# Waits for constant values without a count, in a four-layer graph network on one core

## The chip, the cores and the metric

The kernel runs on 1 core of one Trainium2 chip. The metric is the device time of one execution in microseconds. It is taken on runs of the kernel as it is; one more execution is profiled, and its trace gives all rows below.

## The reference

12,500 nodes with 48 features each, 400,000 edges sorted by destination, with 48 features and a weight each. Four residual layers, each on `h = max(layernorm(x), 0)`:

```
x += segment_sum(edge_weight * h[src -> gathered at dst], src) @ W + bias      # L0: gather at dst, sum by src
x += (1 + eps) * h + segment_sum(relu(h[src] + edge_attr), dst)                # L1: gather at src, sum by dst
x += A (A h)          # L2: A = D^-1/2 (edges + loops) D^-1/2, by src, two passes
x += A' h             # L3: the same normalised adjacency, transposed
```

## The kernel before, in words

Every engine has its own instruction stream, written out by hand, and streams meet only through semaphores. The fast path has four stages.

Stage A (60 to 5,900 us of the span) reads the edges once and sorts them. A chunk K (53 of them) is 60 columns of 128 edges, in three slots s of 20 columns. For each slot TensorE counts edges per block of 128 source nodes (`count`, L2174), gathers node features (`pick`, two halves, L2186) and ranks edges in their block (`rank`, four quarters, L2195 and L2197). VectorE weighs the gathered features into `rec` (`weigh`, L1737), reads the ranks (`highest`, L1732) and computes each edge's place (`positions`, L1754). GpSimd then scatters the 20 columns of `rec` to the DRAM table `recB` with 20 indirect DMAs (`scatter`, L1420), one for each 128 edges. Buffers `rec`, `qpos` are three deep, one for each slot number; `slot_free` (L1340) waits for the scatters of slot (K-1, s) before slot (K, s) is written.

Beside this, the buckets of the chunk before (10 groups g of 10 blocks) are read back. TensorE sums messages by node (L2212 to L2216) and counts pairs of nodes into a dense matrix, in five pieces for each group (`bucket`, L2204; the matmuls into `pT`, L2230 and L2234, two banks in turn, piece e waits for the copy of piece e-2). ScalarE copies each piece to `stg` (L2585) after a wait on `e_ca` (L2584), and after five copies stores them with a DMA (L2590). SyncE loads the buckets, features and rows with DMAs of its own.

The loops over K, s and g of stage A are unrolled in Python, so that all their wait values are constants. GpSimd's scatters are interrupted by waits on TensorE: `paced` (before columns 2, 4, 6, ... of a slot, on piece numbers by the table `PACE`) and `ranked` (before two or three columns, on `e_rk`, by `RANKED`). These two, and the waits on positions, weights, edge rows and prefilled memory at the head of `scatter`, all go through `hold`.

Stage B (5,915 to 7,240 us) is layer 1 on the sorted edges: TensorE gathers and sums, VectorE adds and makes one-hots, ScalarE and GpSimd split numbers into three bf16 pieces. Its loop over K is a hardware loop on all engines but TensorE, so its waits are mostly against register values. Stages C and D (7,240 to 9,072 us) are dense matmuls with the counted adjacency (`dense`, L2332, with `hold` on the loaded columns; `product`, L2362).

`hold` (L230) is called where an engine must wait before its next step: on GpSimd in `scatter`; on ScalarE in `make_dT`, `bucket`, `meta`; on SyncE before nearly every DMA; on VectorE in `slot_free`; on TensorE in `dense`. Other waits in the file are `wait_ge` alone, through `reached` (L1346) or directly. `general_...` functions are a slow path for other inputs that isn't run here.

Of the kernel before, what the change touches and what calls it, by code (L numbers as in the profile page):

```python
# [92 lines left out]
def build(nc, x, src, dst, ea, ew, weight, bias, eps, out):  # L93
    with ExitStack() as ctx:
# [3 lines left out]
        def sem(name):  # L98
            return ctx.enter_context(nc.semaphore(name))
# [84 lines left out]
        s_hold = sem("s_hold")  # L184
# [44 lines left out]

        def hold(eng, sem_, val):  # L230

            eng.wait_ge(sem_, val).then_inc(s_hold, 1)

        def cols(ap, i, g):
            return ap[:, bass.ds(i * TL + g * G, G)]
# [51 lines left out]
        def general_gpsimd(p):  # L287
# [23 lines left out]
            with p.If(fl):  # L311
                with p.Fori(0, MI) as i:
                    for g in range(L):
                        n = i * L + g
                        p.wait_ge(f_st, n * 2 + 2)
                        hold(p, f_ea, n * 16 + 16)
                        for k in range(G):
                            p.indirect_dma_start(recT, bass.IndirectOffsetOnAxis(ap=posi[:, g, k:k + 1], axis=0),
                                                 rows[:, g, k * RW:(k + 1) * RW], None).then_inc(s_fd, 16)
                        p.wait_ge(s_fd, n * 80 + 80)  # L320
                        p.sem_inc(f_sc, 1)
# [7 lines left out]
            with p.Fori(0, NI) as i:  # L329
                for g in range(L):  # L330
                    n = i * L + g
                    p.wait_ge(b_msg, n + 1 + L)
                    p.wait_ge(b_rc, n + 1)
                    hold(p, b_pi, n + 1)
                    for k in range(G):
                        p.indirect_dma_start(recN, bass.IndirectOffsetOnAxis(ap=posi[:, g, k:k + 1], axis=0),
                                             rows[:, g, k * RW:(k + 1) * RW], None,
                                             bounds_check=E - 1, oob_is_err=False).then_inc(s_cr[g], 16)
# [11 lines left out]
            def gather(k, i, g):  # L350
                S, q = WHICH[k]
                if S is main:
                    q -= 1
                hold(p, S["ix"], (i + q * NI) * L + g + 1)
                for c in range(G):
                    p.indirect_dma_start(gb[:, g, c * D:(c + 1) * D], None, tab[k],
                                         bass.IndirectOffsetOnAxis(ap=posi[:, g, c:c + 1], axis=0)
                                         ).then_inc(S["g"][g], 16)
# [696 lines left out]
        val = pha("val", [128, SB], F32)  # L1055
# [1953 lines left out]
```

## Time and profile before

| | |
|---|---|
| median of 3 runs | 9079.17 us (9056.56 to 9087.81) |
| profiled execution | 9074.16 us |
| its span | 9072.3 us |
| stage A, 60 to 5,855 us | 5795 us of it |
| TensorE busy | 6311.8 us (70%), 98,024 matmuls |
| VectorE, ScalarE, GpSimd busy | 57%, 40%, 46% |
| granted TensorE clock, mean of the span | 0.79 |

A line of the profile page's digits shows the span in 40 slices, and each digit is the busy share of a slice in tenths:

```profile
PE   5555555555555555555555555579999899999999
...
POOL 2455555555555555555555555568888600000000
PEclk6677666676666667666666676799999999999999
```

In the rows an engine's name with a q (ACTq, SPq, POOLq) is its sequencer: waits, branches and the issue of DMAs. "remote" and "another core or an unknown queue" stand for a wait whose end the profile can't tie to an instruction; the kernel has one core, so no other core is meant.

### The profile page before, as it was taken

How to read it: one execution, taken by the hardware profiler on the slowest of the kernel's cores; microseconds unless marked ns; L12 is line 12 of the kernel's file. 1: busy time of each engine (PE TensorE's matmuls, PEld its weight loads, DVE VectorE, ACT ScalarE, POOL GpSimd, SP SyncE). 2: the span in 40 equal slices, each digit the busy share in tenths (PEclk: the TensorE clock that was granted, in tenths of full speed). 3: DMA queues.
4: the chain of work that ended last, by engine and by line, in shares of the span. 5: the costliest groups of instructions: out<-in, count | busy, mean ns of one | idle time of the engine just before them, and what ended most of it. 6: DMA issues, size and time to landing. Idle time of an engine off the chain costs nothing.

```text
span 9072.3 us, 246452 instructions
## 1 busy us (share of the span) xinstructions
PE 6311.8 (70%) x98024; PEld 5439.8 (60%) x98025; DVE 5135.0 (57%) x7430; ACT 3658.8 (40%) x6626; POOL 4155.1 (46%) x4228
## 2 busy tenths in 40 slices
PE   5555555555555555555555555579999899999999
PEld 4444444444444444444444444468888899999999
DVE  5555555555555555555555555599999911111565
ACT  3444444444444444444444444478888600000000
POOL 2455555555555555555555555568888600000000
PEclk6677666676666667666666676799999999999999
DMA  6666566666666666666665666579999987888998
GB/s 172 186 180 179 177 181 183 183 187 179 190 183 181 177 179 200 182 177 181 191 185 177 185 190 184 162 251 316 316 318 316 306 272 261 283 276 277 283 266 213
DMA packets 1540180, 1969.31 MB, mean 217 GB/s; under 512 B 620045, under 2 KB 1204095, under 8 KB 1538767
## 3 DMA queue, kind: packets, MB, share of 16 engines
q1 hardware_dynamic: 1064800, 1272.38, 47.4%
q10 hardware_dynamic: 374342, 523.47, 18.5%
q0 software_dynamic: 100000, 158.60, 5.6%
q8 instruction: 776, 12.71, 0.6%
q14 instruction: 262, 2.15, 0.1%
HBM read 1335.36 MB, written 618.65 MB: 215 GB/s over the span
## 4 chain that ended last, share of the span: by engine, by line
PE 41%; another core or an unknown queue 17%; issue 13%; DVE 12%; ACT 10%; ACTq 2%; DMA 2%; POOL 2%; SPq 0%; DVEq 0%; POOLq 0%
PE pG L2347 9%; PE pT L2230 7%; PE pG L2374 7%; ACT stg L2585 5%; PE pT L2234 3%; PE pG L2186 3%; DVE doh L1724 2%; PE pT L2347 2%; ACT dfar L2552 2%; PE pR L2347 2%; DVE msum L1936 2%; PE pG L2197 2%; PE pG L2195 1%; PE pG L2311 1%
## 5 line engine op out<-in xcount | busy, mean ns | idle before, releaser
L1420 POOL DMA_INDIRECT recB<-rec,qpos x3125 | 3071.8, 983 | 2782.7 <-PE pT L2230 1376.0
L2230 PE MATMUL pT<-soh,doh 128*128 128x128 bf16 x10600 | 1820.9, 269 | 1608.3 <-ACT stg L2585 1317.4
L2585 ACT CAST stg<-pT 128x512 fp8e4<-128x512 f32 x2650 | 1497.7, 585 | 1977.5 <-PE pT L2230 1147.4
L2230 PEld LDWEIGHTS pT<-soh,doh 128*128 128x128 bf16 x10600 | 1042.5, 118 | 1867.8 <-ACT stg L2585 1421.5
L2234 PE MATMUL pT<-car,qidb 128*128 128x256 fp8e4 x2597 | 932.9, 359 | 32.5 <-issue 32.0
L1732 DVE TENSOR_REDUCE val<-pG 128x5 f32<-128x490 f32 x628 | 417.6, 665 | 878.7 <-PE pG L2197 385.4
L1737 DVE TENSOR_TENSOR rec<-pG,wN 128x480 f32<-128x480 f32 x314 | 206.6, 658 | 1173.2 <-remote 1053.1
L2311 PE MATMUL pG<-mpl,doh 128*128 128x144 bf16 x10388 | 765.9, 227 | 38.6 <-POOL mpl L1471 28.7
L1724 DVE TENSOR_TENSOR doh<-dm,pG 128x2560 bf16<-128x2560 bf16 x530 | 783.7, 1479 | 3.0 <-ACT dm L2671 2.6
L1724 DVE TENSOR_TENSOR doh<-smd,pG 128x2560 bf16<-128x2560 bf16 x530 | 783.4, 1478 | 0.0
L1724 DVE TENSOR_TENSOR soh<-smd,pG 128x1280 bf16<-128x1280 bf16 x530 | 432.5, 816 | 514.9 <-PE pT L2230 376.8
L2311 PEld LDWEIGHTS pG<-mpl,doh 128*128 128x128 bf16 x10388 | 666.8, 96 | 68.6 <-POOL mpl L1471 52.4
L2195 PE MATMUL pG<-ohA,qlt 128*128 128x490 bf16 x628 | 307.0, 489 | 562.1 <-DVE val L1732 435.0
L2374 PE MATMUL pG<-xq,yt 128*128 128x144 bf16 x9800 | 615.7, 226 | 13.0 <-DMA xq<-hS 8.6
L2374 PEld LDWEIGHTS pG<-xq,yt 128*128 128x128 fp8e4 x9800 | 615.0, 98 | 13.6 <-issue 8.8
L1468 POOL TENSOR_TENSOR mpl<-mpl 128x480 f32<-128x480 f32 x530 | 523.5, 988 | 200.8 <-ACT mpl L2696 198.0
L1476 POOL MEMSET xi<- 64x512 bf16 x1 | 0.5, 519 | 1221.0 <-PE pT L2347 1221.0
L2010 DVE TENSOR_REDUCE ysC<-pG 128x144 f32<-128x432 f32 (+1 forms) x50 | 24.6, 541 | 938.8 <-PE pG L2347 485.4
L2299 PE MATMUL pG<-xp,sT 128*128 128x48 bf16 x15582 | 485.1, 183 | 101.8 <-ACT sT L2686 52.3
L1471 POOL TENSOR_TENSOR mpl<-mpl 128x480 f32<-128x480 f32 x530 | 523.6, 988 | 41.4
L2556 ACT ACTIVATE dT<-dfar,qonf 128x1280 bf16<-128x1280 bf16 x314 | 427.5, 1362 | 274.4 <-remote 248.1
L2299 PEld LDWEIGHTS pG<-xp,sT 128*128 128x128 bf16 x15582 | 443.9, 96 | 148.4 <-ACT sT L2686 99.6
(265 smaller groups left out, 14180.2 us busy)
## 6 DMA issues: line engine op xcount, KB each, us to landing
recB<-zt ACTq DMA_DIRECT2D x102, 2425.5 KB
brec<-recB SPq DMA_DIRECT2D x477, 495.0 KB
erec<-recB SPq DMA_DIRECT2D x477, 495.0 KB, 5.5
cl<-cA SPq DMA_DIRECT2D x80, 2560.0 KB, 10.9
cA<-stg ACTq DMA_DIRECT2D x530, 320.0 KB
cl<-cA SPq DMA_DIRECT2D x40, 2720.0 KB, 11.2
drow<-dlD SPq DMA_DIRECT2D x157, 640.0 KB
srowB<-srD SPq DMA_DIRECT2D x265, 320.0 KB, 5.9
```

What stands on the lines that cost most here:

```text
L1420: p.indirect_dma_start(recF, bass.IndirectOffsetOnAxis(ap=qpos[:, s, c:c + 1], axis=0), rec[:, s, c, :], None).then_inc(s_sc[s], 16)
L1468: p.tensor_tensor(mpl[:, o, 1, :, :], mpl[:, o, 0, :, :], mpl_u[:, o, 0, :, :, 1], ALU.subtract).then_inc(m_r1, 1)
L1471: p.tensor_tensor(mpl[:, o, 2, :, :], mpl[:, o, 1, :, :], mpl_u[:, o, 1, :, :, 1], ALU.subtract).then_inc(m_pl, 1)
L1724: return v.tensor_tensor(out.rearrange("p b (c two) -> p b c two", two=2), code.unsqueeze(2).to_broadcast([128, n, w // 2, 2]), numbers[:, ...
L2230: ins = t.matmul(bank[:, h * 256 + b * 128:h * 256 + b * 128 + 128], doh[:, o, 2 * e + b, h * 128:(h + 1) * 128], soh[:, o, 2 * e + b, :], ...
L2234: t.matmul(bank[:, 0:256], qidb[:, :], carf[:, r, e * 256:(e + 1) * 256], start=False, stop=True, skip_group_check=True)
L2299: ins = t.matmul(B8[o][:, b * D:(b + 1) * D], sT[:, g % 5, b * 128:(b + 1) * 128], xp[:, g * GB + b, k, :], start=(k == 0), stop=(k == 2))
L2311: ins = t.matmul(B8[2 + 2 * par][:, h * 3 * D:(h + 1) * 3 * D], doh5[:, g % 5, b, h * 128:(h + 1) * 128], mpl_u[:, g % 2, :, b, :, 1], sta ...
L2347: ins = t.matmul(B8[4 * o + b // 3][:, b % 3 * 3 * D:(b % 3 + 1) * 3 * D], clf[u % 3][:, k, b * 128:(b + 1) * 128], (xpc, xw)[r][:, k0 + k ...
L2374: ins = t.matmul(B8[o][:, w * 3 * D:(w + 1) * 3 * D], ytf[o][s][:, n, w * 128:(w + 1) * 128, b], xq[:, FIRST[s] + n, b, :], start=(s == 0 ...
L2556: a.activation(dT[:, half], dfar[:, :], ACT.Relu, bias=qonf[:, 0:1], scale=-1.0).then_inc(e_dT, 1)
L2585: a.copy(stg[:, o, :, e * 256:(e + 1) * 256], B8[6 + (g * 5 + e) % 2][:, :].rearrange("p (h x) -> p h x", h=2), saturate=False).then_inc(e ...
```

## The change

`hold` so far made a wait that also adds 1 to the semaphore `s_hold` when it is over. Nothing waits for `s_hold`. Now this is so only where the value is held in a register; where it is a Python integer, the wait is a `wait_ge` like the others, with nothing added. All calls, values and their order stay, `paced` and `ranked` on GpSimd among them.

```diff
         def hold(eng, sem_, val):
 
-            eng.wait_ge(sem_, val).then_inc(s_hold, 1)
+            if isinstance(val, int):
+                eng.wait_ge(sem_, val)
+            else:
+                eng.wait_ge(sem_, val).then_inc(s_hold, 1)
```

The callers that matter most:

```
def paced(K, s, c):
    back, g = SUMMED[s][1]
    hold(p, e_ca, ((K - back) * JG + g) * 5 + PACE[s][c])
...
for e in range(5):                                  # ScalarE, bucket
    hold(a, e_ca, c * 5 + (e + 1))
    a.copy(stg[...], B8[6 + (g * 5 + e) % 2][...]).then_inc(e_cv, 1)
hold(a, e_cv, c * 5 + 5)
a.dma_start(cA[...], stgB[...]).then_inc(s_cs[o], 16)
```

## Rows read from the trace of the kernel before

**Rows 1.** Windows, three stages: span, busy time (instructions) per engine, granted clock, DMA share, GB/s.

```profile
60.00:5855.00 5795.00, 3262.42 (x42267) 2475.19 (x42267) 3167.79 (x5216) 2545.97 (x4879) 3070.30 (x3124) 0.68 0.62 181
...
5915.00:7240.00 1325.00, 1179.90 (x26127) 1103.13 (x26128) 1309.46 (x1431) 1039.28 (x1607) 1049.36 (x1062) 0.98 0.94 307
7240.00:8470.00 1230.00, 1213.92 (x19375) 1213.20 (x19372) 216.52 (x368) 14.28 (x26) 1.50 (x3) 1.00 0.86 273
```

**Rows 2.** Chain of waits from 60 to 5900 us: share of it by line.

```profile
by line: another core or an unknown queue 26.2%; issue 14.2%; PE pT L2230 11.4%; ACT stg L2585 7.3%; PE pT L2234 4.1%; PE pG L2186 4.0%; ACT dfar L2552 3.7%; PE pG L2197 2.5%; PE pG L2195 2.2%; DVE doh L1724 2.0%; PE pG L2174 1.8%; DVE rm L
```

**Rows 3.** Waits from 60 to 5900 us: who waited for whom, us, times, longest.

```profile
POOL recB L1420 <- PE pT L2230: 1376.0, 472, 8.7
...
ACT stg L2585 <- PE pT L2230: 1146.2, 1357, 9.4
...
DVE rec L1737 <- remote: 1053.1, 188, 10.7
...
ACT hs L2539 <- remote: 405.8, 87, 7.1
...
DVE val L1732 <- remote: 384.0, 74, 11.2
```

**Rows 4.** Waits of the held line 232 on its own: kind, count, ns min/median/max, stretch.

```profile
L232 ACTq EVENT_SEMAPHORE  x4447: 17/17/1392, 42.4 to 5914.1; - x194
L232 SPq EVENT_SEMAPHORE  x3941: 2/17/4119, 68.5 to 8416.4; - x198
L232 POOLq EVENT_SEMAPHORE  x2260: 17/17/17, 78.2 to 5841.7; - x189
...
L232 PEldq EVENT_SEMAPHORE  x138: 51/51/164, 7227.6 to 8431.1; - x138
```

**Rows 5.** The copies as a group (page, part 5); one beside TensorE (timeline).

```profile
L2585 ACT CAST stg<-pT 128x512 fp8e4<-128x512 f32 x2650 | 1497.7, 585 | 1977.5 <-PE pT L2230 1147.4
...
3052.89 0.42 PE L2230 MATMUL pT<-soh,doh 128*128 128x128 bf16 x2
...
3053.42 0.58 ACT L2585 CAST stg<-pT 128x512 fp8e4<-128x512 f32 x1 [3.21 <-PE pT L2230]
```

**Rows 6.** ScalarE, VectorE and TensorE where the wait has no count.

```profile
3051.04 1.38 PE L2186 MATMUL pG<-hw,dT 128*128 128x48 bf16 x30
...
3052.46 0.66 DVE L1737 TENSOR_TENSOR rec<-pG,wN 128x480 f32<-128x480 f32 x1 [0.34 <-PE pG L2186]
...
6498.45 0.65 DVE L1936 TENSOR_TENSOR msum<-pG,erec 128x480 f32<-128x480 f32 x1
...
6499.14 0.60 ACT L2696 ACTIVATE mpl<-msum 128x480 f32<-128x480 f32 x1 [0.95 <-DVE msum L1936]
...
6499.82 0.99 POOL L1468 TENSOR_TENSOR mpl<-mpl 128x480 f32<-128x480 f32 x1 [0.59 <-ACT mpl L2696]
```

**Rows 7.** GpSimd and ScalarE released by one matmul, and the pick beside them.

```profile
1988.83 0.93 PE L2186 MATMUL pG<-hw,dT 128*128 128x48 bf16 x30
...
1988.74 1.07 ACT L2585 CAST stg<-pT 128x512 fp8e4<-128x512 f32 x2 [0.92 <-PE pT L2230]
...
1989.43 0.96 POOL L1420 DMA_INDIRECT recB<-rec,qpos  x1 [1.07 <-PE pT L2230]
```

**Rows 8.** The run of scatters from 3040 us, and what starts after it.

```profile
3041.74 1.38 PE L2186 MATMUL pG<-hw,dT 128*128 128x48 bf16 x30
...
3046.43 0.96 POOL L1420 DMA_INDIRECT recB<-rec,qpos  x1 [0.30 <-issue]
3048.64 0.66 DVE L1737 TENSOR_TENSOR rec<-pG,wN 128x480 f32<-128x480 f32 x1 [9.92 <-remote]
```

**Rows 9.** Head of a slot: positions written, then the first scatter.

```profile
3028.54 0.18 DVE L1754 TENSOR_TENSOR qpos<-posf,nowhere 128x20 int32<-128x20 f32 x1
...
3030.01 0.95 POOL L1420 DMA_INDIRECT recB<-rec,qpos  x1 [3.80 <-issue]
```

**Rows 10.** Chain of waits over the span, by engine (the page).

```profile
PE 41%; another core or an unknown queue 17%; issue 13%; DVE 12%; ACT 10%; ACTq 2%; DMA 2%; POOL 2%; SPq 0%; DVEq 0%; POOLq 0%
```

## The prediction

> **What bounds the kernel now.** I read the windows first. Stage A takes 5795 of 9072 us, and there no engine is full: TensorE is busy 3262 us, GpSimd 3070, VectorE 3168, at a granted clock of 0.68 [rows 1]. In stage B VectorE is busy 1309 of 1325 us, in stage C TensorE 1214 of 1230 [rows 1]. So a change in how engines hand work to one another can show in stage A, and hardly elsewhere.
>
> Second, the chain of waits of stage A. 26.2% of its 5840 us, 1530 us, is "an unknown queue", 7.3% (426 us) are ScalarE's copies L2585, 14.2% is "issue", the time between a release and a start [rows 2]. The list of waits tells what the unknown part is: VectorE waits 188 times for L1737, 74 times for L1732 and ScalarE 87 times for L2539, together 349 waits and 1843 us, mean 5.3 us [rows 3]. All three wait for TensorE's matmuls. A close look shows such a case: the 30 matmuls of a `pick` end at 3041.74 + 1.38 = 3043.12, yet the VectorE operation that waits for them starts at 3048.64, 2.21 us after the start of the last scatter of a run on GpSimd that had begun before [rows 8]. When GpSimd stood still the same step took 0.04 us (matmuls end at 3052.42, VectorE starts at 3052.46) [rows 6]. So a signal of TensorE that falls into a run of scatters is often told only when the run is over. I don't know by which path; but it says what the `paced` and `ranked` waits do, they break the runs, and it makes the start of each run matter.
>
> (1) ScalarE's copies. With a hold: TensorE's last matmul of a piece ends at 3052.89 + 0.42 = 3053.31, the copy starts at 3053.42, 0.11 us [rows 5]. Without: 0.04 us on VectorE after `pick` and 0.04 us on ScalarE itself after VectorE (6499.10 to 6499.14) [rows 6]. The hop gets 0.07 us shorter. The chain holds 426 / 0.585 = 728 copies (585 ns is their mean [rows 5]). If all of them were released by TensorE, that is 51 us; before 1357 of the 2650 ScalarE stood idle for it [rows 3, 5], 51%, which gives 26 us. I take 40.
>
> (2) GpSimd's paced scatters. A single matmul releases ScalarE, which starts 1988.74, and GpSimd, which starts 1989.43, 0.69 us later [rows 7]; with ScalarE's own 0.11 us the hop is 0.80 us. Of it 0.30 us stand before every scatter, waiting or not [rows 8]. GpSimd's hop without a count, on an arithmetic instruction, is 0.08 us (6499.74 to 6499.82) [rows 6]. The trace shows no indirect DMA with a wait of its own, so the saving lies between 0 and 0.80 - 0.08 = 0.72 us. I take 0.80 - 0.30 - 0.08 = 0.4. What is it worth? 1530 us of unknown waits at 5.3 us are some 290 on the chain. Each ends with a run, and the run ends earlier by what it starts earlier, if its start is what was late. GpSimd waited for a piece of TensorE 472 times [rows 3], and I take it that for half of the 290 such a start is what was late: 290 x 0.4 x 0.5 = 58, I take 60. Ends: 0 and 290 x 0.72 = 209 us.
>
> The Trainium skill, Perfetto Trace Analysis, section on GPSIMD's SWDGE instructions, says that the sequencer pushes such an instruction into a wait queue with its wait and is then free to decode the next. By that rule the whole decoding of a scatter could be over before its wait is, and the sum would take the upper end of (2) rather than its middle. No row of this trace has that case; an indirect DMA never carries a wait here.
>
> (3) Heads of slots. At a head six holds stand in a row on GpSimd for s = 0 and four for s = 1, 2. The positions are ready at 3028.72, the first scatter starts at 3030.01, 1.29 us, 0.49 more than (2) has for one hold [rows 9], so 0.1 us for each of five further ones. Half of them go, 0.25 us, at 157 heads 39 us, and 0.4 us more at each by (2), 63 us. But GpSimd is only 2% of the chain [rows 10], and in two of three slots (the run before still goes on) the waits are over long before. I take 15; ends 0 and 80.
>
> (4) DMAs issued on ScalarE. Before each store of a group there is a hold on the copies. ACTq is 2% of the chain [rows 10], 181 us, at 0.38 us an issue some 470; 0.07 us each is 33 us. The instructions between the wait and the DMA stay. I take 20; ends 0 and 33.
>
> (5) At nothing: SyncE's holds (3941) shorten every load by 0.06 us or so, but SPq is 0% of the chain [rows 10]; if its loads ran late, 0.06 us on 530 bucket loads would be 32 us. VectorE's waits on free slots, and TensorE's 138 in stage C, where matmuls already issued cover them (TensorE is busy 1214 of 1230 us [rows 1]); without the cover 138 x 0.07 = 10 us. In stage B almost all held values are in registers and stay as they are. The 8600 or so updates of `s_hold` that go away are waited for by nobody.
>
> **Sum.** 40 + 60 + 15 + 20 = 135 us. These hops run beside others that are nearly as late: a copy that comes 0.07 us sooner may then wait for a landing or for the end of a run. I take a quarter off: 101 us. 9074 - 101 = 8973 for the profiled execution, and 9079 - 101 = 8978 against the median, which lies 5 us above it: 8975. All upper ends together (51 + 209 + 80 + 33) would give 8706.
>
> **Rivals.**
>
> *Scatters start sooner and catch more signals (slower).* The pacing tables count TensorE's pieces, and what lies between a piece and the start of a scatter is the 0.80 us of part (2). With 0.4 us less, the `pick`, `rank` or `count` that TensorE does right after the piece ends inside the run more often. The case is there: a `pick` runs from 1988.83 to 1989.76, and the run of scatters that a piece before it released began at 1989.43, 0.33 us before its end [rows 7]. The price of one signal caught is a scatter and a half, 1.3 to 2 us; more where the run is long, as the 5.5 us of [rows 8]. If each chunk catches two more, at 1.7 us, that is 53 x 2 x 1.7 = 180 us, less the 75 of parts (1), (3) and (4): 9079 + 105 = 9184. It decides from about one more caught signal a chunk (90 us) on. For it: the 1530 us of unknown waits are of this kind. Against it: the runs also end sooner, and many signals are already caught.
>
> *Absorbed (no change).* The ends of runs set the beat of stage A, and ScalarE's 0.07 us wait for it like the rest. If GpSimd's hop stays as it is, only a small part of (1) and (4) is left, 20 us: 9059. For it: 26% of the chain ends with a run. Against it: 7.3% are copies, which wait for no run.
>
> *The waits stay instructions of their own (the change doesn't do what it says).* Then 17 ns each and the updates alone go: 9070 to 9079. Against it: waits without a count start 0.04 us after the release in three rows [rows 6].
>
> *The whole of GpSimd's hop goes (faster still).* Part (2) at its upper end and runs broken at better places: 9079 - 250 = 8829.
>
> **How the numbers follow.** Within 0.3% (27 us) a measurement of this kernel can't be told from no change. Chances: forecast 0.50 (8880 to 9040), more signals caught 0.26 (9110 to 9260), absorbed 0.15 (9045 to 9085), waits stay 0.02, faster still 0.07. Faster: 0.50 + 0.07 + 0.04 of the absorbed = 0.61; no change 0.13; slower 0.26. The likeliest case's own range is 8880 to 9040; the range for all is 8830 to 9160, which leaves out some 0.03 below and 0.17 above.
>
> **What would show it right or wrong.** The list of waits on line 232 shrinks by most of its 10,800 entries. ScalarE's L2585 starts 0.04 us after a piece, not 0.11. The hop from ScalarE's start to GpSimd's at one release shrinks from 0.69 to about 0.3 us. "Unknown queue" falls by 40 to 60 us in stage A and stages B to D keep what they have (9072 - 5915 = 3157 us). If GpSimd's hop has shrunk and the unknown waits have grown in number or length, the first rival holds; if neither L2585's hop nor GpSimd's has changed, I was wrong about what a count costs. A stage B or C that moves by over 20 us would mean that I looked at the wrong place.

## The result: 9083 to 8921 us, and the profile after

The changed kernel takes 8920.94 us in the median of 4 runs (8911.64 to 8932.20); the kernel before took 9083.49 beside it (4 runs). The ratio is 0.9826 [0.9801, 0.9851], 162.6 us less. In a second set beside other kernels it was 8925.15 against 9085.96, ratio 0.9829 [0.9806, 0.9852], 160.8 us less. Forecast were 8975 us, from a gain of 101 us. Direction and range were right, and the gain was 1.6 times the forecast one.

The profiled span went from 9072.3 to 8913.6 us, 158.7 less. First the windows of the changed kernel (columns as in [rows 1]):

```profile
60.00:5700.00 5640.00, 3206.33 (x42245) 2438.38 (x42245) 3171.17 (x5216) 2548.73 (x4877) 3068.27 (x3118) 0.69 0.63 186
...
5760.00:7080.00 1320.00, 1177.75 (x26094) 1098.87 (x26095) 1307.11 (x1429) 1040.53 (x1608) 1048.72 (x1062) 0.98 0.94 308
7080.00:8310.00 1230.00, 1216.10 (x19410) 1215.36 (x19407) 216.24 (x370) 15.23 (x28) 1.50 (x3) 1.00 0.86 274
```

Against [rows 1] stage A is 155 us shorter (5640, not 5795) with the same busy time on VectorE, ScalarE and GpSimd; stage B lies within 5 us of before and stage C has the same 1230. The ends of these windows are chosen by hand. A mark that isn't is ScalarE's last held wait, at 5914.1 us in [rows 4] and at 5759.9 below. So 154 of the 158.7 us are gained before it, and they are idle time of stage A.

What is left of the held line, and what the waits that stay take (columns as in [rows 4]; the wait without a count is line 233 now, the one on a register's value line 235; lines behind `hold` moved down by 3):

```profile
L233 ACTq EVENT_SEMAPHORE  x856: 17/17/1704, 41.6 to 5759.9; - x172
L233 SPq EVENT_SEMAPHORE  x642: 14/17/28, 90.8 to 7091.6; - x161
L233 POOLq EVENT_SEMAPHORE  x365: 17/43/27977, 63.8 to 5669.2; - x183
L233 PEldq EVENT_SEMAPHORE  x29: 51/51/6985, 7070.4 to 8231.5; - x29
...
L235 SPq EVENT_SEMAPHORE  x1689: 17/17/17, 5815.9 to 8257.8; - x188
```

All 2650 copies now have a wait of their own, where before none had; of the 3125 indirect DMAs 1685 have one, where before a single one had (the prediction took it for none). ScalarE's fell most, by 3591, from 4447 to 856; its copies, of which each had one, are 2650.

The timeline where one matmul releases both engines (start, us, engine, line, operation, and in brackets the idle time before):

```profile
560.76 0.42 PE L2233 MATMUL pT<-soh,doh 128*128 128x128 bf16 x2
...
561.22 0.59 ACT L2588 CAST stg<-pT 128x512 fp8e4<-128x512 f32 x1 [0.42 <-PE pT L2233]
...
561.46 0.96 POOL L1423 DMA_INDIRECT recB<-rec,qpos  x1 [3.23 <-PE pT L2233]
```

TensorE ends at 561.18, ScalarE starts 0.04 us later, and GpSimd 0.24 us behind ScalarE, where [rows 7] had 0.69. Over all such cases, from the record of the semaphore to the start, the median hop of a copy went from 113 to 23 ns, and that of a scatter from 686 to 265 ns.

The chain of waits from 60 to 5750 us, by line, and the list of waits from 60 to 5900 us (columns as in [rows 3]):

```profile
by line: another core or an unknown queue 22.1%; issue 16.7%; PE pT L2233 12.4%; PE pT L2237 4.5%; PE pG L2189 4.5%; ACT stg L2588 4.3%; DVE doh L1727 4.2%; ACT dfar L2555 2.9%; PE pG L2200 2.5%; PE pG L2198 2.3%; DVE rm L1780 1.9%; DVE val
```

```profile
POOL recB L1423 <- PE pT L2233: 1360.0, 528, 8.6
ACT stg L2588 <- PE pT L2233: 1075.0, 1269, 7.6
DVE rec L1740 <- remote: 929.8, 170, 8.6
...
DVE val L1735 <- remote: 500.2, 100, 7.8
ACT hs L2542 <- remote: 452.3, 96, 7.3
```

22.1% of 5690 us are 1257 us of unknown waits on the chain; [rows 2] had 1530. But the three late waits of [rows 3] are 366 now and 1882 us, where before they were 349 and 1843. So their number and their length did not fall; only fewer of them lie on the one chain that the view follows. All waits for "remote" together went from 724 and 3108 us to 799 and 3062 us. ScalarE's copies on the chain went from 426 to 245 us, and "issue" rose from 829 to 950. A chain's shares move from one line to another when near ties turn, and their differences are no savings of those lines.

### The profile page after: what moved, and what is told of

Same layout as the page of the kernel before. It is cut to its first block, busy times and chain, and to the rows that moved or that the text cites. A ratio compares the mean times of both kernels' runs of the same rounds, so it can differ in the third digit from the quotient of the medians.

```text
span 8913.6 us, 239230 instructions
## 1 busy us (share of the span) xinstructions
PE 6258.1 (70%) x98024; PEld 5402.8 (61%) x98025; DVE 5136.8 (58%) x7430; ACT 3664.5 (41%) x6626; POOL 4157.3 (47%) x4228
## 4 chain that ended last, share of the span: by engine, by line
PE 43%; issue 16%; DVE 15%; another core or an unknown queue 14%; ACT 7%; ACTq 2%; DMA 1%; POOL 1%; SPq 0%; DVEq 0%; POOLq 0%
PE pG L2350 9%; PE pT L2233 8%; PE pG L2377 7%; DVE doh L1727 4%; PE pT L2237 3%; PE pG L2189 3%; ACT stg L2588 3%; PE pT L2350 2%; DVE msum L1939 2%; PE pR L2350 2%; ACT dfar L2555 2%; PE pG L2200 2%; PE pG L2198 1%; DVE rm L1780 1%
## 5 line engine op out<-in xcount | busy, mean ns | idle before, releaser
L2233 PE MATMUL pT<-soh,doh 128*128 128x128 bf16 x10600 | 1786.7, 266 | 1394.4 <-ACT stg L2588 824.2
```

Of the source, the lines that this page charges most:

```text
L2233: ins = t.matmul(bank[:, h * 256 + b * 128:h * 256 + b * 128 + 128], doh[:, o, 2 * e + b, h * 128:(h + 1) * 128], soh[:, o, 2 * e + b, :], ...
```

## Experiments

**One engine's share at a time.** Four kernels with the changed `hold`, each for some engines only. The kernel before took 9070.03 us beside them (17 runs).

```
-            if isinstance(val, int):
+            if isinstance(val, int) and eng.engine == mybir.EngineType.Activation:      (first)
+            if isinstance(val, int) and eng.engine == mybir.EngineType.Pool:            (second)
+            if isinstance(val, int) and eng.engine not in (... Activation, ... Pool):   (third)
+            if isinstance(val, int) and eng.engine != mybir.EngineType.Pool:            (fourth)
```

> Only ScalarE's constant waits lose their count; GpSimd, SyncE, VectorE and TensorE keep theirs. Theory H (hops: each engine's shorter hop is worth what lies of it on the chain, and the shares add up): 728 copies on the chain at 0.09 us and the DMA issues behind them give 60 to 90 us, so 8995 to 9025. Theory P (GpSimd alone sets the beat of stage A by its runs of scatters, the rest is absorbed): within 25 us of before, 9060 to 9085. Theory N (the new interleaving of runs and TensorE's signals made most of the gain, by luck of places): any value, no reason for additivity.

ScalarE alone: 8955.36 us, ratio 0.9871 [0.9841, 0.9900], 115 us less. That is more than theory H has (60 to 90) and far from theory P's 25.

> Only GpSimd's constant waits lose their count. Theory H: 60 to 80 us, 9005 to 9025. Theory P: nearly the whole gain, 130 to 160 us, 8920 to 8955. The hop from a matmul's signal to the scatter should be 0.27 us as in the changed kernel, against 0.69 before.

GpSimd alone: 8942.39 us, 0.9852 [0.9828, 0.9876], 128 us less: inside P's range, but P fell with the run before.

> Only SyncE's, VectorE's and TensorE's constant waits lose their count. Both theories H and P: 0 to 20 us, 9060 to 9085. If it is over 30 us, loads issued by SyncE were on the chain though the profile gave SPq 0%.

SyncE, VectorE and TensorE: 9018.63 us, 0.9946 [0.9928, 0.9963], 51 us less, over the 30 that the expectation set as its mark. I had priced these at nothing. 3941 of their 4243 holds are SyncE's. With the change the load of a bucket is issued 17 ns after the signal of TensorE that it waits for, before 78 ns (medians), and the carry's load 0.10 us sooner (some 0.78 to 0.68 us in this kernel).

> All constant waits but GpSimd's lose their count. Theory H: the sum of the ScalarE and the rest runs, 60 to 110 us, 8975 to 9025; with the GpSimd run it should add up to the whole 159 us. Theory P: within 30 us of before. Theory N: no sum.

All but GpSimd: 8901.00 us, 0.9813 [0.9789, 0.9836], 169 us less, outside what H (60 to 110) and P (within 30) allow. The three shares add up to 115 + 128 + 51 = 294 us, and the whole is worth 161 to 163. All but GpSimd, 115 + 51 = 166 by sum, gives 169: those two add up. The overlap lies between them and GpSimd: beside the others GpSimd's waits add nothing, and beside GpSimd's 128 the others add some 34 of their 166. GpSimd with one of the others alone was not run.

**The paced waits and the heads.** These and the two below ran in a set in which the kernel before took 7418.16 us (28 runs, 7408.02 to 7430.87), though nothing in it is changed, so they are read by their ratio alone; their expectations were written for 9070. The changed kernel itself was not run in this set.

```
+        def counted(eng, sem_, val):
+            eng.wait_ge(sem_, val).then_inc(s_hold, 1)
...
-                hold(p, e_ca, ((K - back) * JG + g) * 5 + PACE[s][c])
+                counted(p, e_ca, ((K - back) * JG + g) * 5 + PACE[s][c])
-                hold(p, e_rk, (mcnt(K, s) + 1) * 4 + RANKED[s][c])
+                counted(p, e_rk, (mcnt(K, s) + 1) * 4 + RANKED[s][c])
```

> The changed kernel, but GpSimd's paced and ranked waits keep their count (the heads of slots don't). GpSimd alone was worth 128 us, all but GpSimd 169 us, all together 163 us: so GpSimd's part is worth nothing on top of the rest. Theory C (two opposite halves: shorter heads of slots gain, earlier starts of paced runs catch signals and cost): faster than all but GpSimd's 8901, 8850 to 8885. Theory F (a floor: something else ends last once any of the shares is taken): 8890 to 8925 like the two others.

Measured: 7402.17 us, 0.9979 [0.9970, 0.9988].

The same with `counted` at the four holds and the zero-fill hold of a slot's head:

> The changed kernel, but the four or six waits at the head of each slot on GpSimd keep their count (paced and ranked waits don't). Theory C: slower than all but GpSimd, 8930 to 8970. Theory F: 8890 to 8925.

Measured: 7402.71 us, 0.9980 [0.9971, 0.9989]. Both, each short of the full change by one part, are some 16 us faster than before. The two can't be told apart there, and theories C and F stay untested. The traces show why: in this set 3117 and 3119 of the 3124 steps from one scatter to the next are the plain 0.30 us. GpSimd scatters from end to end of stage A, 3125 times 1.26 us or 3950 of its 4140, and the other engines are ready before it. Its waits are over when it comes to them, so what one costs can't show; in the kernel before of [rows 3] it stood idle 472 times for a piece.

**The hop of the copies made longer**, in the kernel before:

```
                 for e in range(5):
+                    hold(a, e_ca, c * 5 + (e + 1))
                     hold(a, e_ca, c * 5 + (e + 1))
```

> The kernel before with ScalarE's counted wait before each of the 2650 copies made twice: the hop from a matmul to a copy grows by one more instruction, some 0.08 us, as much as the change took away. ScalarE alone gained 115 us where the hop on the chain accounts for 66 at most. Theory H (hops, linear): 40 to 70 us slower, 9110 to 9140. Theory M (the same hop is multiplied by the signals that fall into scatter runs): 90 us or more slower, over 9160. Theory P (absorbed): within 20 us of before.

Measured: 7425.27 us beside 7418.16, 1.0008 [0.9998, 1.0017]. That the hop did get longer is in the trace: its median is 204 ns, not 113. By the text above this is theory P, but in a set where GpSimd alone fills stage A (3118 of 3124 steps are 0.30 us), so it says nothing of the first result.

**No pacing**, in the changed kernel:

```
-                    if pace and c in PACE[s]:
-                        paced(K, s, c)
-                    if pace and following and c in RANKED[s]:
-                        ranked(K, s, c)
```

> The changed kernel without the paced and ranked waits on GpSimd, so that a slot's 20 scatters run as one. If TensorE's signals are really held up by runs of scatters: slower by 100 us or more (over 9020), and the unknown waits of VectorE and ScalarE grow. If they are not, and the scatters are only late themselves: faster, 8750 to 8880.

Measured: 7395.38 us, 0.9969 [0.9957, 0.9981], the fastest kernel of this set, by 7 us. Neither expectation was near. Where are the 1650 us that this set lacks? Waits of this kernel from 60 to 4190 us, and its windows:

```profile
POOL recB L1419 <- issue: 941.6, 3088, 0.3
...
ACT stg L2584 <- PE pT L2229: 338.0, 699, 7.3
...
DVE val L1731 <- PE pG L2196: 299.6, 254, 4.9
ACT hs L2538 <- PE pG L2173: 193.4, 154, 4.9
```

```profile
60.00:4185.00 4125.00, 2801.70 (x42333) 2211.95 (x42333) 3132.08 (x5222) 2511.41 (x4886) 3076.98 (x3124) 0.79 0.84 255
4250.00:5500.00 1250.00, 1129.37 (x25156) 1054.49 (x25157) 1241.59 (x1358) 999.80 (x1550) 1009.54 (x1027) 0.99 0.95 310
```

Stage A takes 4125 us with as many instructions, and there is no "remote" wait at all. The first line is GpSimd's plain step of 0.30 us, 3088 times. The kernel before with its copies' hold doubled, of this set too, looks the same. So the unknown waits on which the prediction built are not a property of the kernel alone.

**The same questions where the waits are late.** The last set, of the changed kernel, the fourth kernel of above (all but GpSimd), the doubled hold and the kernel without pacing, ran beside a kernel before of 9085.96 us (14 runs, 9047.53 to 9101.67).

> The changed kernel itself, on a chip whose own time for the kernel before tells how late TensorE's signals come there. Theory of amplification (a few hundred late waits on TensorE's signals in stage A turn each saved hop into more than itself): where the kernel before takes about 9070 us, ratio 0.980 to 0.985 as first measured; where it takes about 7418 us, the late waits are missing and the ratio is 0.996 to 0.999, 7 to 30 us. Theory of plain sums (hops on a chain that always counts, 101 us forecast): 0.989 at 9070, and 101 / 7418, a ratio of 0.986, on the other chip.

Measured: 8925.15 us, 0.9829 [0.9806, 0.9852], the first result again. It lies in the range of the theory of amplification, but that range was taken from the first result, so it speaks for the repeat and not for the theory. It leaves out the 0.989 of plain sums.

> As the changed kernel, but GpSimd's constant waits keep their count. If GpSimd's share, 75 us forecast in two parts, comes on top of the others', this is 50 to 75 us slower than the changed kernel beside it. If the shares stand in for each other (115, 128 and 51 us alone, some 160 together), it is within 25 us of it. Where the kernel before takes 7418 us, both theories shrink to a tie within 0.2%.

Measured: 8921.82 us, 0.9820 [0.9795, 0.9846], 3 us from the changed kernel beside it. GpSimd's median hop is 686 ns in this kernel and 265 ns in the changed one, so 0.42 us on each released scatter buys nothing once the other engines' waits are short.

> The kernel before with one more counted wait ahead of each of ScalarE's copies of stage A, some 1,360 of them of about 0.07 us. By the sum, at most 95 us and by its share of the chain about 40 us slower: ratio 1.004 to 1.010. If what the late signals do multiplies a hop, 60 to 120 us slower (1.007 to 1.013) where the kernel before takes 9070 us, and 1.001 where it takes 7418 us (where this edit gave 1.0008).

Measured: 9105.81 us, 1.0024 [0.9998, 1.0050], 20 us more, between a gain of 2 and a loss of 45, for 0.09 us more at 2650 copies (median 204 ns). That is less than both expectations have. A hop that the late signals multiply would have been 60 us or more, so for the hop of the copies that theory falls; for the others it is not tested.

> The changed kernel without GpSimd's waits on TensorE's picks and ranks. The rival of my prediction had it that scatters which start sooner catch more of the late signals. Where the kernel before takes 9070 us: by that rival, 60 to 200 us slower than the changed kernel; if the waits only cost, 0 to 30 us faster. Where it takes 7418 us few signals are late and both say 0.1 to 0.3% faster than the changed kernel.

Measured: 10332.76 us, 1.1379 [1.1350, 1.1407]: 1408 us slower than the changed kernel, from the same edit that made it faster in the other set. Neither expectation was near. The waits of this kernel from 60 to 7110 us, and the last part of a run of twenty scatters:

```profile
POOL recB L1419 <- DVE qpos L1753: 3023.1, 150, 76.7
ACT stg L2584 <- remote: 2969.9, 494, 12.0
...
PE pT L2229 <- ACT stg L2584: 2301.1, 551, 11.5
```

```profile
3001.14 0.42 PE L2229 MATMUL pT<-soh,doh 128*128 128x128 bf16 x2
...
3001.45 0.95 POOL L1419 DMA_INDIRECT recB<-rec,qpos  x1 [0.31 <-issue]
...
3007.76 0.96 POOL L1419 DMA_INDIRECT recB<-rec,qpos  x1 [0.30 <-issue]
3008.48 0.58 ACT L2584 CAST stg<-pT 128x512 fp8e4<-128x512 f32 x1 [7.80 <-issue]
...
3012.81 0.96 POOL L1419 DMA_INDIRECT recB<-rec,qpos  x1 [0.30 <-issue]
3016.95 1.07 ACT L2584 CAST stg<-pT 128x512 fp8e4<-128x512 f32 x2 [7.88 <-remote]
```

The piece is done at 3001.56 and its copy starts at 3008.48, 6.9 us later, while five more scatters start. It starts with the run still going on: the signal doesn't wait for its end. Each such piece holds up TensorE, whose two buffers for pieces are full, then the positions of the next slot, for which GpSimd now waits 150 times and 3023 us. The same program in the other set, in the middle of a run of scatters too:

```profile
2500.04 0.96 POOL L1419 DMA_INDIRECT recB<-rec,qpos  x1 [0.30 <-issue]
...
2500.42 0.42 PE L2229 MATMUL pT<-soh,doh 128*128 128x128 bf16 x2
...
2500.87 0.58 ACT L2584 CAST stg<-pT 128x512 fp8e4<-128x512 f32 x1 [0.30 <-PE pT L2229]
2501.30 0.95 POOL L1419 DMA_INDIRECT recB<-rec,qpos  x1 [0.30 <-issue]
```

Done at 2500.84, copied from 2500.87 on, 0.03 us, with scatters at the same spacing of 1.26 us. So TensorE's signals come late beside scatters in one condition and not in the other. The paced waits are worth 1408 us in the first and cost some 7 us in the second, by the two kernels that kept nearly the whole change.

This can be counted over stage A, from the end of a matmul that signals to the next update of its semaphore. In the kernel before, 3054 such matmuls end while a run of scatters goes on, and 1869 of these signals (61%) come over 0.3 us late; 1225 end while GpSimd stands still, and 81 (7%) are late. The late ones are 1.7 us late in the median and 11 at most; in this set's kernel without pacing the median is 4.2 us. Of VectorE's and ScalarE's own signals 12 are late. In the set of 7418 us 65 of 4173 are late without pacing. In the changed kernel 1817 of 2996 are late beside scatters, about as many as before.

## Why the prediction was right, and where its terms were wrong

**Where it shows: right.** Stage A, but for some 5 us; stages B and C as they were.

**Parts (2) and (3), GpSimd: right in size per hop, wrong in worth.** Forecast were 60 + 15 = 75 us. Alone they give 128. Beside the other engines' they give 3 us less than nothing, inside what can be told (their intervals are some 22 us to each side). So 75 was too little for this part alone, and adding it to the others' failed: once the rest comes sooner, GpSimd's starts bring nothing more (and once they come sooner, the rest brings little). That "half of the 290" unknown waits hang on such a start is shown by no run. Something was absorbed, but not what the `Absorbed` rival named: it had ScalarE's hops wait for the ends of the runs.

**Parts (1) and (4), ScalarE: mis-sized.** Forecast 40 + 20 = 60 us, measured 115 alone. Part (1) by itself can't carry that: the same 0.09 us added to the copies cost 20 us, 45 at most. At most 2650 of ScalarE's 3591 holds that went stood at copies; I priced the 941 or more others only where they stand before a store, and nothing for the rest. The trace has 0.09 us at the store of a group (252 to 165 ns, median; 530 stores) and 0.18 us from a copy of a piece to the copies of a slot's numbers into `rec` behind it (776 to 592 ns, with ScalarE's share alone). Which of them brings the rest, or whether a saved hop gives more than an added one costs, no run tells apart; this is open.

**Part (5), SyncE: failed.** "At nothing" was read off a chain with SPq at 0%. Measured are 51 us for the three engines of that part. The chain books a load's lateness on what it follows, a DMA, "issue" or the unknown queue, not on the engine that issued it late. The text had the number for the other case, 32 us, and gave it no place in the sum. That it is SyncE and not TensorE or VectorE is argued, from 3941 of 4243 holds, and not tested alone.

**The quarter off: too little, and in the wrong place.** The shares overlap by (294 - 161) / 294 = 45%, and the overlap is not spread: ScalarE's and SyncE's add up in full, and it is GpSimd's share and theirs that stand in for each other. The sum fell in the range because two terms were too small (60 for 115, 0 for 51) and one too large (75 for about 0 beside the others), which is partly luck. Without the quarter it would have been 135, nearer to the 161 to 163 measured.

**The rival on the other side: not set off by this change.** Late waits of the three kinds went from 349 to 366, and from 1843 to 1882 us, 39 us more and not the 180 that it asked for. By the prediction's own sign (GpSimd's hop shorter, the unknown waits grown in number or length) the rival would hold, and yet the kernel got faster. The sign had no size, and failed. That it was worth a chance is shown by the kernel without pacing: scatters that wait for no piece at all, and not 0.4 us less, cost 1408 us.

**Unknown waits "fall by 40 to 60 us": unsure.** On the chain they fell by 273 us and in the list of waits they didn't fall. The forecast named a view that can't carry it.

## What to carry to other kernels

Don't put a count on a wait that nobody reads: on this kernel it cost 0.09 us at each hop of ScalarE, 0.06 to 0.10 us at SyncE's loads and 0.42 us ahead of an indirect DMA that stood waiting. Where GpSimd was never waiting, nearly all of the change was worth 16 us of 7418. When a change touches several engines, price each alone, and then ask which of them the others make worthless; engines with 0% of the chain (SyncE, with a few waits of VectorE and TensorE) can still be worth 51 us. And where a wait's cause is "unknown", ask whether it is the kernel's at all before an edit is judged by it: the kernel without pacing was 0.3% faster than before in one set of runs and 14% slower in another.

## What was not expected of the hardware

The same kernel took 7418 us in one set of 28 runs and 9039 to 9102 us in all the others that were run for this, though the 28 runs and the last 14 were on the same chip. The difference lies in stage A (4125 us without pacing, against 5795 of before and 7050 without pacing), where the granted clock was 0.79 to 0.81 in one and 0.62 to 0.69 in the other; stages B and C differ by little. With the late signals GpSimd's indirect DMAs keep their spacing of 1.26 us, and most of TensorE's signals beside them come late. The path of this is open, and that the late signals make up the whole difference of the two sets is not shown. The fetching of instructions doesn't order the kernels. Its first queue moved 776 or 777 packets in all of them; its second moved 262 packets before, 206 after and 206 without pacing, 1408 us apart, and 282 with the hold doubled, in either set.

```profile
q14 instruction: 206, 1.69, 0.1%
```

What sets the one condition or the other was not found.
